# Vision-transformer block on one core: key transfers as two-dimensional copies on the sync queue, layer normalisations applied by ScalarE

## What is computed

```python
def _layernorm(x, axis=-1, eps=1e-05):
    m = jnp.mean(x, axis=axis, keepdims=True)
    v = jnp.var(x, axis=axis, keepdims=True)
    return (x - m) / jnp.sqrt(v + eps)

h = _L0_tok_ref(x, W, b, class_token, pos_embed)             # (64, 197, 192)
h = h + _L0_attn_ref(_layernorm(h), w_qkv, w_proj, b_proj)   # 12 heads of 16, keys n-6 .. n+6
h = h + _L0_ffn_ref(_layernorm(h), router_w, w1, b1, w2, b2) # softmax router, top 2 of 8, gelu
```

## Time and profile before

| what | value |
|---|---|
| time, median of 3 runs | 1888.35 us (1887.83 to 1889.15) |
| the profiled execution: its time | 1887.49 us |
| the profiled execution: its span in the trace | 1885.7 us |
| busy over the span | PE 87%, DVE 66%, POOL 59%, ACT 41% |
| mean granted clock of TensorE | 0.936 |
| images in the attention part | 64 |

### The profile page before, as it was taken

One profiled execution on the slowest core, in us unless ns is written; L12 is line 12 of the kernel. 1 busy time (PEld: TensorE's weight loads), 2 busy tenths in 40 slices (PEclk: granted clock), 3 DMA queues, 4 the chain that ended last, 5 costly groups with the idle time before them and its releaser, 6 DMA issues. The chain is left out here.

```text
span 1885.7 us, 57924 instructions
## 1 busy us (share of the span) xinstructions
PE 1635.0 (87%) x19910; PEld 1361.4 (72%) x19911; DVE 1237.3 (66%) x3136; ACT 772.1 (41%) x1339; POOL 1104.6 (59%) x1020
## 2 busy tenths in 40 slices
PE   5668989888989798889898509999999999999995
PEld 4567878777868687778786406777777777777774
DVE  3567677677767677677676635666666666666663
ACT  2444444444434344344344305444444444444441
POOL 3226777767767677677677653455555555555554
PEclk8879999999999999999998759999999999999998
DMA  5453444444444444444444233443443444444332
GB/s 184 149 169 94 110 108 118 110 95 111 116 95 116 106 100 110 104 109 119 95 113 126 69 88 91 63 58 61 61 63 57 62 62 58 61 61 63 56 48 30
DMA packets 223375, 172.99 MB, mean 92 GB/s; under 512 B 142590, under 2 KB 197088, under 8 KB 222176
## 3 DMA queue, kind: packets, MB, share of 16 engines
q1 hardware_dynamic: 120752, 100.80, 20.5%
q0 software_dynamic: 74544, 42.61, 16.8%
q10 hardware_dynamic: 27904, 27.14, 4.8%
HBM read 94.76 MB, written 65.08 MB: 85 GB/s over the span
## 5 line engine op out<-in xcount | busy, mean ns | idle before, releaser
L376 POOL DMA_INDIRECT sorted_scratch<-payload,place x256 | 414.6, 1620 | 68.0 <-issue 67.3
L970 POOL DMA_INDIRECT out<-y,token x219 | 369.0, 1685 | 73.8 <-issue 73.2
L1078 PE MATMUL down<-w_hi,g_hi 128*128 x1314 | 323.6, 246 | 1.9 <-DVE y L1044 1.1
L1080 PE MATMUL down<-w_hi,g_lo 128*128 x1314 | 323.0, 246 | 0.0
L1079 PE MATMUL down<-w_lo,g_hi 128*128 x1314 | 322.9, 246 | 0.0
L756 PE MATMUL near<-we,patches 128*100 128x192 f32 x1536 | 279.2, 341 | 33.0 <-issue 24.6
L756 PEld LDWEIGHTS near<-we,patches 128*100 128x100 f32 x1536 | 256.6, 174 | 48.6 <-issue 45.9
L1066 PE MATMUL up<-e_xT,w_hi 128*128 128x384 f16 x1314 | 286.0, 327 | 0.2 <-ACT act_out L991 0.2
L991 ACT ACTIVATE act_out<-up,bias 128x384 f32<-128x384 f32 x438 | 251.2, 582 | 72.3 <-PE up L1066 72.2
L983 ACT COPY e_xT<-turned 128x1152 f16<-128x1152 f16 x73 | 81.7, 1119 | 362.6 <-PE turned L1058 362.6
L1027 DVE TENSOR_TENSOR g_lo<-act_out,g_hi 128x768 f16<-128x768 f32 x219 | 209.9, 959 | 7.6
(11 more groups left out here) (154 smaller groups left out, 3218.1 us busy)
## 6 DMA issues: line engine op xcount, KB each, us to landing
patches<-in_xt SPq DMA_DIRECT2D x64, 600.0 KB
rows<-sorted_scratch SPq DMA_DIRECT2D x73, 301.5 KB, 2.8
v_diag<-v_scratch SPq DMA_DIRECT2D x192, 78.1 KB
v_scratch<-v_rows SPq DMA_DIRECT2D x64, 159.4 KB
stage<-in_w ACTq DMA_DIRECT2D x8, 1152.0 KB
k_diag<-qk SPq DMA_DIRECT2D x512, 12.5 KB
out<-h ACTq DMA_DIRECT2D x64, 75.0 KB
out<-h ACTq DMA_DIRECT2D x64, 72.8 KB
```

What stands on the lines that cost most here:

```text
L376: pool.indirect_dma_start(out=sorted_dram, out_offset=bass.IndirectOffsetOnAxis(ap=at, axis=0), in_=payload[0:rows, 2 * image + n, :], in_ ...
L970: pool.indirect_dma_start(out=out, out_offset=bass.IndirectOffsetOnAxis(ap=token[k][:, n:n + 1], axis=0), in_=y[k % 2][:, n, :], in_offset ...
L1078: pe.matmul(dst, g_hi[k % 2][:, m, cols], high, start=(m == 0), stop=False)
L1080: ins = pe.matmul(dst, g_lo[k % 2][:, m, cols], high, start=False, stop=(m == MF - 1))
```

## The change

Three things change, all in `attention_part`.

1. The transfers of all 12 heads into `k_diag` are issued by SyncE. The four of heads 8 to 11 leave ScalarE's queue, with their wait for `max_set`.
2. `qk16` and `k_diag` are laid out with the high and the low half of a row side by side, and both tiles have the same row length of 222. A transfer takes one run of 222 + 200 = 422 elements per partition (high half, zeros, low half) where it took two runs of 200. The writes and the matmuls that use these tiles keep their number and shape and get other strides.
3. `normalise` moves from VectorE to ScalarE, as `xn = rs * h + off`, with the scale and the offset read from memory, in two activations. VectorE makes `off = -mean * rs` (`shift_of`, one instruction on 100 x 2 elements) where it normalised. On ScalarE the second normalisation stands behind the exponential and the first behind the copy of the values. The overwriting of `h2` now waits for ScalarE's normalisation of the image before.

```diff
-        qk16 = [sb(f"qk16_{k}", [128, 2, 3, QUERY_WIDTH], F16) for k in range(2)]
-        k_diag = sb("k_diag", [128, 2, HEADS, KEY_WIDTH], F16)
+        qk16 = [sb(f"qk16_{k}", [128, 3, 2, KEY_WIDTH], F16) for k in range(2)]
+        k_diag = sb("k_diag", [128, HEADS, 2, KEY_WIDTH], F16)
...
-                    for h in range(8):
-                        to = DH * h
-                        sp.dma_start(k_diag[to:to + DH, :, h, REACH:REACH + SPAN],
-                                     qk16[(k - 3) % 2][to:to + DH, :, 1, 0:SPAN]).then_inc(s["k_diag_set"], 16)
+                    both = KEY_WIDTH + SPAN
+                    for h in range(HEADS):
+                        chunk, at = (1, DH * h) if h < 8 else (2, 64 + DH * (h - 8))
+                        to = DH * (h % 8)
+                        halves = qk16[(k - 3) % 2][at:at + DH, chunk].rearrange("p w n -> p (w n)")
+                        sp.dma_start(k_diag[to:to + DH, h].rearrange("p w n -> p (w n)")[:, REACH:REACH + both],
+                                     halves[:, 0:both]).then_inc(s["k_diag_set"], 16)
...
+            def normalise(h, rs, off, xn, number, n_th):
+
+                act.wait_ge(s["offset" + number], n_th)
+                need(act, s["lo" + number], n_th - 1)
+                for n in range(2):
+                    ins = act.activation(xn[:, n, :], h[:, n, :], ACT.Identity, bias=off[:, n:n + 1], scale=rs[:, n:n + 1])
+                ins.then_inc(s["normed" + number], 1)
...
-                if runs(t, 2):
-
-                    if runs(t, 3):
-                        act.wait_ge(s["max_set"], 2 * a)
-                    else:
-                        act.wait_ge(s["qk_lo_set"], a + 1)
-                    for h in range(8, HEADS):
-                        to = DH * (h - 8)
-                        act.dma_start(k_diag[to:to + DH, :, h, REACH:REACH + SPAN],
-                                      qk16[k % 2][64 + to:64 + to + DH, :, 2, 0:SPAN]).then_inc(s["k_diag_set"], 16)
...
+                    normalise(h2, rs2, off2, xn2, "2", b + 1)
                     act.wait_ge(s["normed2"], b + 1)
...
+                    normalise(h1[k], rs1, off1, xn1, "1", f + 1)
                     act.wait_ge(s["normed1"], f + 1)
...
-            def normalise(h, mv, rs, xn, number, n_th):
+            def shift_of(mv, rs, off, number, n_th):
 
                 dve.wait_ge(s["rstd" + number], n_th)
-                need(dve, s["lo" + number], n_th - 1)
-                for n in range(2):
-                    ins = dve.tensor_scalar(xn[:, n, :], h[:, n, :], mv[:, n, 0:1], rs[:, n:n + 1], ALU.subtract, ALU.mult)
-                ins.then_inc(s["normed" + number], 1)
+                need(dve, s["normed" + number], n_th - 1)
+                dve.scalar_tensor_tensor(out=off[:], in0=mv[:, :, 0], scalar=-1.0, in1=rs[:], op0=ALU.mult, op1=ALU.mult)\
+                   .then_inc(s["offset" + number], 1)
...
                     need(dve, s["h2_out"], 32 * d)
+                    need(dve, s["normed2"], d)
```

More of the change, by code:

```diff
@@ L199, in attention_part @@
         rs1 = sb("rs1", [ROWS, 2], F32)
+        off1 = sb("off1", [ROWS, 2], F32)
         xn1 = sb("xn1", [ROWS, 2, D], F32)
@@ L231, in attention_part @@
         rs2 = sb("rs2", [ROWS, 2], F32)
+        off2 = sb("off2", [ROWS, 2], F32)
         xn2 = sb("xn2", [ROWS, 2, D], F32)
@@ L252, in attention_part @@
         counts = mixed[0:ROWS, 2 * VCOLS:2 * VCOLS + 5 * EXPERTS].rearrange("p (n e) -> p n e", e=EXPERTS)
-        names = ("first_in tab_set load_c zero_mem pad_set weights embedded h1_set stats1 aggr1 rstd1 normed1 hi1 lo1 turned1 xT_set qk_done "
+        names = ("first_in tab_set load_c zero_mem pad_set weights embedded h1_set stats1 aggr1 rstd1 offset1 normed1 hi1 lo1 turned1 xT_set qk_done "
                  "qk_hi_set qk_lo_set k_diag_set v_done v_set v_out v_in norm_done o_hi_set "
                  "max_set scored shifted exp_set prob_turned p_set "
-                 "o_lo_set o_turned oT_set proj_done h2_set stats2 aggr2 rstd2 normed2 hi2 lo2 den_set "
+                 "o_lo_set o_turned oT_set proj_done h2_set stats2 aggr2 rstd2 offset2 normed2 hi2 lo2 den_set "
                  "pv_done var1 var2 setup1 setup2 turned2 xT2_set routed logit_set step weighed marks_set counted staged split_hi split_lo h2_out "
@@ L500, in body @@
                     need(act, s["scored"], 2 * (g - 1))
-                    act.copy(qk16[(k - 1) % 2][:, 0, :, 0:SPAN], qk[:, 0:3, 0:SPAN]).then_inc(s["qk_hi_set"], 1)
+                    act.copy(qk16[(k - 1) % 2][:, :, 0, 0:SPAN], qk[:, 0:3, 0:SPAN]).then_inc(s["qk_hi_set"], 1)
                     act.wait_ge(s["v_done"], g + 1)
@@ L624, in body @@
                 if runs(t, 5):
-                    normalise(h2, mv2, rs2, xn2, "2", b + 1)
+                    shift_of(mv2, rs2, off2, "2", b + 1)
                 if due_7:
@@ L637, in body @@
                 if runs(t, 0):
-                    normalise(h1[k], mv1, rs1, xn1, "1", f + 1)
+                    shift_of(mv1, rs1, off1, "1", f + 1)
                 if isinstance(t, int) and t == 0:
@@ L655, in body @@
                     dve.wait_ge(s["qk_hi_set"], g + 1)
-                    dve.tensor_tensor(qk16[(k - 1) % 2][:, 1, :, 0:SPAN], qk[:, 0:3, 0:SPAN], qk16[(k - 1) % 2][:, 0, :, 0:SPAN],
+                    dve.tensor_tensor(qk16[(k - 1) % 2][:, :, 1, 0:SPAN], qk[:, 0:3, 0:SPAN], qk16[(k - 1) % 2][:, :, 0, 0:SPAN],
                                       ALU.subtract).then_inc(s["qk_lo_set"], 1)
@@ L875, in body @@
                                         dst = scores[32 * w:32 * w + 32, n, heads.start * KEYS:heads.stop * KEYS]
-                                        ins = pe.matmul(dst.rearrange("p (h c) -> p h c", c=KEYS), qk16[k % 2][:, of_q, chunk, at:at + 32],
-                                                        k_diag[:, of_k, heads, at:at + KEYS], start=False, stop=closes)
+                                        ins = pe.matmul(dst.rearrange("p (h c) -> p h c", c=KEYS), qk16[k % 2][:, chunk, of_q, at:at + 32],
+                                                        k_diag[:, heads, of_k, at:at + KEYS], start=False, stop=closes)
                         ins.then_inc(s["scored"], 1)
```

## The result

The changed kernel takes **1947.12 us** (median of 4 runs, 1939.29 to 1951.61) against 1888.74 us for the kernel before beside it. The ratio is **1.0305, 95% interval 1.0272 to 1.0339**: slower by 58 us. The forecast was 1836, with 1808 to 1880 as its range, so it was wrong in sign. Rival B gave 1940.

What follows compares the result with a forecast made beforehand. The prediction took TensorE's wait for the exponential, delayed by ScalarE's key issues, as the bound. Gains of 46 us (22 E bodies x 2.1) and 6 us (first eight images) made 52 us: 1836 us forecast, range 1808 to 1880.

Steps and rivals of the forecast that it cites:

- Rival B: SyncE's twelve issues stretch under load, keys late by 2.2 us in E and 1.6 in C: 1940 us; chance 0.10.
- What bounds the kernel: Attention part, 400 to 1000 us: TensorE waits 34.1 us for ScalarE's exponential, which sits behind key-transfer issues.
- E: TensorE body without the routing count, embedding start to next: 15.6 us, including 2.18 us waiting for the exponential.
- Edit 1: Four key transfers leave ScalarE; the exponential can start at the end of the shift, 1.73 us sooner.
- Edit 2: SyncE issues twelve key transfers, 5.8 to 7.7 us against 5.1; just in time in E, hidden in C.
- C: TensorE body that runs the routing count, embedding start to next: 13.7 us, with no wait worth a name.
- The second price: Patch load behind SyncE's keys, issued 2.6 us later: costed at nothing, 0.7 us per C (22 us) kept for the range.
- Edit 3: Normalisations move to ScalarE, 0.9 us a pair; first has slack, second tile's path grows 1.4 to 2.4; VectorE gains 1.0.
- Rival A: Half a gain: GpSimd's order holds back VectorE's 1.0 us lead; 1864 us, chance 0.22.
- Rival C: ScalarE is the wrong engine for the normalisations: 480 ns against VectorE's 389, 23 to 30 us; 1917 us, chance 0.04.
- D: Nothing changes: something else releases the exponential and the label "issue" misleads; 1888 us, chance 0.06.
- The sum: E becomes 13.9 to 14.0 us; 22 bodies x 2.1 = 46 us, plus 6 in the first eight images: 52 us.

Runs made afterwards that it cites:

- e12: Kernel before plus new key layout, patch load ahead of keys, ten keys on SyncE, two on ScalarE behind the exponential; normalisations stay on VectorE: 1835.91 us, ratio 0.9763.
- e13: e12 with eight key transfers on SyncE and four on ScalarE behind the exponential and the high half: 1885.57 us, ratio 0.9999.
- e3: e2, but SyncE issues eight key transfers and ScalarE still issues four, ahead of the exponential: 1879.47 us, ratio 0.9966.
- e2: Kernel before with only the key edit: new layout and runs, all twelve transfers on SyncE, normalisations on VectorE: 1937.16 us, ratio 1.0271.
- e4: Changed kernel with the patch load moved ahead of the key transfers in SyncE's body: 1925.48 us, ratio 1.0190.
- e17: e12 with SyncE's patch load back behind the key transfers: 1864.33 us, ratio 0.9894.
- e23: e15 with only the first normalisation on ScalarE, the second back on VectorE: 1858.75 us, ratio 0.9857.
- e15: e12 with both normalisations on ScalarE, as in the change: 1882.58 us, ratio 0.9997.
- e19: e15 plus a wait: GpSimd makes the first tile's low half only after VectorE's routing steps: 1854.13 us, ratio 0.9819.
- e11: e4, and SyncE waits until the keys have landed before it issues the transfers of v: 1946.31 us, ratio 1.0352.
- e16: e4, and GpSimd's scatter of the second tile starts only behind a wait for the key transfers: 1937.87 us, ratio 1.0280.
- e1: Kernel before with only the normalisations moved to ScalarE, key transfers unchanged: 1977.15 us, ratio 1.0474.
- e9: e1 plus a wait: in bodies with routing, GpSimd makes the first tile's low half only after VectorE's routing steps: 1953.48 us, ratio 1.0356.
- e14: e12 with eleven key transfers on SyncE and one on ScalarE behind the exponential: 1886.55 us, ratio 1.0006.

## Why the prediction was wrong

**What bounds the kernel: right for E, and not the whole of it.** The waits for the exponential came from the issues ahead of it. With them gone, the median E takes 14.0 us in the changed kernel and 14.1 in e12; the sum said 13.9 to 14.0. But e13 takes these issues out of the way too, has no wait for keys, and gains nothing: the waits come back at ScalarE's copies, and its median E stays at 16.4 us. That e12 has the predicted number, 1835.91 us, is chance: it leaves the normalisations alone, and more than half of its gain is the patch load's place (1.3 of 2.4%), which the prediction costed at nothing.

**Edit 1: right.** The exponential starts 0.03 to 0.04 us after the shift's end in the 54 bodies from 150 to 1050 us. The rule of the Trainium skill (DMA: Bandwidth & Descriptors, "Issuing engines are not separate DMA queues") that issuing from several engines saves only sequencer time, usually small, would have made this edit worth nothing. Here who issues four of the twelve is worth 57 us (e3 against e2), about as much as the whole change costs.

**Edit 2: the step that failed.** For C the text called the keys "hidden": issues from 1.0 us on, done at 8.7, landed by 11.5, wanted at 11.7. At the medians of the 20 waits they start at 1.1, are issued by 10.1, land at 15.2 and are wanted at 10.95; in the body shown it is 2.75 + 8.76 + 6.99 = 18.5 us, wanted at 671.66 - 660.69 = 11.0. So C takes 19.1 us at the median and not 13.7. Three terms were mis-sized. The landing was taken as "at most the 2.8 us of a load of 301.5 KB"; the view gives 2.8 us as the median of such loads, in the expert part, and where TensorE waits it is 3.0 to 7.0 us. The price per issue was right at the median of all, 0.589 us, but twelve take 8.9 us in these bodies against 7.7. And the keys are wanted 0.7 us earlier. The second price, "I cost it at nothing" for patches, came out as 22 us for the change (e4) and 25 us in e17. The text kept 22 us for the range, from 0.7 us per C; the sum is the same by luck, since the waits for patches are 28, of 2.0 us on average.

**Edit 3: the other failed step.** The pair on ScalarE was sized nearly right: 0.98 us, and 537 ns for one, where the sum took 0.9 and 0.48. What failed is "All that VectorE does later in C, and so the maxima in E, comes 1.0 us sooner" and "the pair for the first normalisation has slack". VectorE does get a lead and loses it beside GpSimd. In the median C from 150 to 1050 us, its steps from the first `scaled<-chosen,tmp` to the end of the second copy run from 8.3 to 12.4 us into the body in the kernel before, from 7.6 to 11.7 in e2 (the key edit alone), and from 7.0 to 12.7 in the changed kernel: by the normalisations they start 0.6 us sooner and end 1.0 us later. The path of the first normalisation has no slack (e23, 18 us): its high half comes behind the copy's start, and the low half behind it is what passes VectorE. Rival A named "GpSimd's order holds it" but priced it as a gain not had. By e15 against e12 the normalisations are a loss of 44 us, and by e19 against e15 34 us of that go with GpSimd's order.

**Rival B: right place, price near.** It said 1940 and a wait of the score matmuls for a key transfer; 1947 and 90.7 us of such waits over the attention part came. It was to decide "from 0.72 us per issue on". At the median of all issues that is not reached, but the twelve of the bodies in which TensorE waits take 8.9 / 12 = 0.74 us each. B had the landing too short as well, from the same 2.8 us, and put more of the lateness in E (2.2 us) than in C (1.6 us), where E has 2 of the 20 waits. Its price leaves out edit 3's loss, so its nearness is partly luck. B had 0.10, although the text's own working already had the keys 0.4 us late in E (12.45 against 12.1) and called that in time. **Rival C** (ScalarE the wrong engine, 0.04) had the sign right for this edit, by 23 to 30 us of longer instructions; most of the loss came from order. **D** is excluded by the changed kernel itself: without the issues the exponential starts with the shift's end.

**The sum** took the two edits as independent gains on one path. Alone they cost 2.7% (e2) and 4.7% (e1), together 3.05%.

**Open.** Why the last keys land 1.2 us after their issue in one body and 4 to 7 us in the next. What SyncE issues behind them is excluded (e11). GpSimd's scatters run beside slow landings, but beside those of 1.2 us in e11 too, and e16 did not separate the two. That e1 alone (+4.7%) costs twice what the same edit costs on top of e12 (+2.3%) fits an exponential that is already late there; this was not tested apart.

## What to carry to other kernels

Moving issues off one queue is only half an edit: work out, for the queue that receives them, when the last transfer has landed and not only when it was issued. Take the landing from transfers of the same kind amid the same traffic, look whether the view gives a median or a bound, and treat a margin of less than its spread as late. Here, with the patch load first, two transfers behind the critical instruction gained 2.4%, and one or four gained nothing; none, with the patch load last, lost 2.7%.

Relieving an engine gains only if what it does next is not held by another. Look up which of its instructions are already longer than their twins of equal size in the profile: a copy at 435 ns that can take 173 is a sign that it stands beside another engine. Then ask in which order the two come out, and what the change delays on the other engine's inputs.

## What the runs showed of the hardware

- Merging two runs of 200 halves into one of 422 did not make the issue noticeably cheaper: 589 ns against 594 at the median. The layout with all else equal is worth 0.3% (e3).
- A 100x4 integer copy on VectorE takes from 173 to 2152 ns, and ends with GpSimd's scatter or with the instruction behind it; its durations in the changed kernel (ns, min/median/max):

```profile
L620 DVE TENSOR_SCALAR payload<-token_at x32: 173/2135/2152, 137.2 to 1162.0; 100x4 uint32<-100x4 f32 x32
```

- Adding a wait to GpSimd (e9, e19) made the kernel 22 and 34 us faster.
- The last of twelve transfers of 13.2 KB between two SBUF tiles landed 1.2 to 6.6 us after its issue (e11, 54 bodies), and up to 7.0 us in the changed kernel. In the window of the longest of these waits, the transfer engines were busy for 0.67 of the time.
- Eleven transfers on SyncE and one on ScalarE took 46 us more than ten and two (e14 against e12).
